# The second layer of a four-layer network: border zeros written earlier, two sampled units interleaved on VectorE, and x read back in four pieces

## The reference, cut to what matters

```python
d = layernorm_over_pixels(conv1x1(depthwise3x3(x[:, :256])))
off = conv3x3(d)                       # 18 channels: y and x shift of 9 taps
samples = bilinear(d, pixel + tap + off)   # four corners, zero outside the image
dc = einsum('bckhw,ock->bohw', samples, dc_w) + dc_b
dc = layernorm_over_channels(dc) * ln_g + ln_b
out = x * (d * sigmoid(dc)) + x * g    # g: a gate per channel from x[:, 256:]
```

## Time and profile before

| | us |
|---|---|
| median of 3 runs | 4316.83 (4311.97 to 4317.98) |
| profiled execution | 4315.14 |
| its span | 4313.3 |
| layer 1, first to last DVE output | 2752.0 to 3467.3 |
| of this the fetches and corner sums | 2900.7 to 3447.4 |

### The profile page before, as it was taken

How to read it: one execution, slowest core, us unless ns; L and a number is a source line. 1 busy time by engine, 2 the same in 40 slices (tenths; PEclk the granted TensorE clock), 3 DMA queues, 4 the chain that set the end, 5 groups by cost and what they waited for, 6 DMA issues and landing times. The chain is left out here.

```text
span 4313.3 us, 67226 instructions
## 1 busy us (share of the span) xinstructions
PE 3912.8 (91%) x18504; PEld 2390.0 (55%) x18504; DVE 2958.2 (69%) x4476; ACT 2583.8 (60%) x4599; POOL 2081.0 (48%) x1857
## 2 busy tenths in 40 slices
PE   5999999999999999999998999788779377969999
PEld 3555555555555555555557777447667242435553
DVE  7888888888888888888875333538888833235562
ACT  5899999999999999999984333222112420113331
POOL 0555555555555555555542555316676500026663
PEclk8999999999999999999999999899899677989999
DMA  1200000000000000000001000229999812453312
GB/s 48 101 10 10 9 9 12 10 9 9 12 10 9 9 12 10 9 9 12 9 24 64 0 0 0 76 82 378 369 370 392 301 46 66 142 133 69 69 40 78
DMA packets 146902, 326.60 MB, mean 76 GB/s; under 512 B 45736, under 2 KB 46760, under 8 KB 145788
## 3 DMA queue, kind: packets, MB, share of 16 engines
q1 hardware_dynamic: 105340, 174.46, 13.0%
q0 software_dynamic: 41472, 151.01, 9.0%
HBM read 246.14 MB, written 79.04 MB: 75 GB/s over the span
## 5 line engine op out<-in xcount | busy, mean ns | idle before, releaser
L559 POOL TENSOR_TENSOR cpb_sum<-cpb_tab 128x512 f32<-128x512 f32 x1028 | 1045.8, 1048 | 964.8 <-DVE cpb_r L689 964.5
L670 ACT ACTIVATE cpb_h<-cpb_z,net_vec 128x512 f32<-128x512 f32 x1536 | 1006.0, 697 | 50.2 <-PE cpb_z L610 37.5
L607 PE MATMUL cpb_z<-cpb_r,cpb_w2a 128*128 128x512 f32 x2048 | 858.2, 419 | 23.4 <-DVE cpb_h L730 23.4
L689 DVE SCALAR_TENSOR_TENSOR cpb_r<-cpb_sum,cpb_r 128x512 fp32r<-128x512 f32 x1024 | 696.2, 710 | 187.4 <-ACT cpb_r L664 187.4
L608 PE MATMUL cpb_z<-cpb_r,cpb_w2b 128*128 128x512 f32 x2048 | 801.3, 391 | 0.0
L610 PE MATMUL cpb_z<-cpb_r,cpb_w2a 128*128 128x512 f32 x2048 | 799.4, 390 | 0.0
L689 DVE SCALAR_TENSOR_TENSOR cpb_r<-cpb_z,cpb_r 128x512 fp32r<-128x512 f32 x1028 | 662.0, 686 | 160.0 <-ACT cpb_r L664 154.3
L664 ACT ACTIVATE cpb_r<-cpb_z 128x512 fp32r<-128x512 f32 x1028 | 560.4, 604 | 127.7 <-PE cpb_z L594 127.7
L664 ACT ACTIVATE cpb_r<-cpb_sum 128x512 fp32r<-128x512 f32 x1024 | 598.4, 648 | 2.0 <-POOL cpb_sum L559 2.0
L607 PEld LDWEIGHTS cpb_z<-cpb_r,cpb_w2a 128*128 128x128 f32 x2048 | 383.7, 187 | 365.9 <-issue 300.9
L1537 DVE SCALAR_TENSOR_TENSOR dc_acc<-dc_g,dc_wt,dc_acc 128x512 f32<-128x512 f32 x560 | 444.9, 800 | 57.5 <-DMA dc_g<-conv_out,dc_idx 37.0
(11 more groups left out here) (345 smaller groups left out, 5206.0 us busy)
## 6 DMA issues: line engine op xcount, KB each, us to landing
conv_out<-dc_ys SPq DMA_DIRECT2D x576, 64.0 KB
cpb_log<-log_dram SPq DMA_DIRECT2D x66, 256.0 KB, 3.1
qk_parts<-gn_r SPq DMA_DIRECT2D x64, 256.0 KB, 2.0
dc_wr<-in_dc_wT SPq DMA_DIRECT2D x9, 1024.0 KB
bias_dram<-cpb_bst SPq DMA_DIRECT2D x520, 8.0 KB
net_x<-in_x SPq DMA_DIRECT2D x8, 1024.0 KB, 9.9
sa_qa<-qk_parts SPq DMA_DIRECT2D x16, 512.0 KB
sa_ka<-qk_parts SPq DMA_DIRECT2D x16, 512.0 KB
```

The lines of the kernel that those rows point to most:

```text
L559: pool.tensor_tensor(SUM[:, r, :].rearrange("p (y x) -> p y x", x=W), TAB[:, slot, r, 0, :].unsqueeze(1).broadcast_to([P, NF // W, W]), TA ...
L607: pe.matmul(z2[:, bank, :], W2A[:], R1[:, k, :], start=True, stop=False)
L670: act.activation(H2[:, t % 8, :], z2[:, t % 3, :], ACT.Relu, bias=V("cpb_b2")).then_inc(h2a, 1)
L689: v.scalar_tensor_tensor(R2[:, t % RING, :], first_layer(t), 0.0, R1[:, t % RING, :].bitcast(F32), ALU.max, ALU.subtract).then_inc(r2_read ...
```

## The change

- The 18 border DMAs leave layer 1. SP issues them in `layer0_mlp`, from a tile of zeros of half the width there (each row is written as two halves), after a memset by POOL, and waits for them at the end of that stage. POOL's wait for the borders before the first fetch goes, and so does the memset of layer 1's ZERO.
- In layer 1 POOL zeroes only the one-pixel ring of DP that the offset convolution reads, in two memsets, instead of all of DP. PE, not ACT, waits for it.
- The four corner steps of a unit (k = 0..3) are issued skewed: in round u DVE issues step 0 of unit u, step 2 of unit u-1, step 1 of unit u, step 3 of unit u-1. Steps 0 to 2 of the first 120 units write their running sum to PSUM (`pn`, four banks), and only step 3 writes ACC. For the last 24 units the sums stay in ACC.
- x comes back in four DMAs of 1 MB: the first when PE is done, the others when 129, 136 and 140 units are sampled.

The core of the diff ("..." marks lines left out):

```diff
@@ layer0_mlp
+        ZERO = s.sb("zero", [P, C // 2])
...
+        @block.sync
+        def _(sp):
+            sp.wait_ge(blank, 1)
+            HP = H + 4
+            edge, gaps = 2 * HP + 2, H - 1
+            for rows in itertools.chain(*g["conv_out"]):
+                for r0 in (0, HP * HP - edge):
+                    sp.dma_start(rows[r0:r0 + edge, :].rearrange("r (k c) -> r k c", k=2),
+                                 ZERO[0:edge, :].unsqueeze(1).broadcast_to([edge, 2, C // 2])).then_inc(borders, 16)
+                middle = rows[edge + W:edge + W + gaps * HP, :].rearrange("(y x) c -> y x c", x=HP)[:, 0:4, :]
+                sp.dma_start(middle.rearrange("y x (k c) -> y (x k) c", k=2),
+                             ZERO[0:gaps, :].unsqueeze(1).broadcast_to([gaps, 8, C // 2])).then_inc(borders, 16)
+            sp.wait_ge(borders, 16 * 18)
...
+            pool.memset(ZERO[:], 0.0).then_inc(blank, 1)
@@ layer1
-            for u in range(SLOTS):
-                for b in range(B):
-                    rows = table[u][b]
-                    sp.dma_start(rows[0:edge, :], ZERO[0:edge, :]).then_inc(borders, 16)
...
             sp.wait_ge(y_mm, TILES)
-            sp.dma_start(X[:].rearrange("p t n -> p (t n)"), x_spill).then_inc(x_back, 16)
-            sp.wait_ge(borders, 16 * 3 * SLOTS * B)
+            for n, units in enumerate((0, LAST[1] + 1, LAST[2] - 4, LAST[3] - 4)):
+                cols = slice(n * NF, (n + 1) * NF)
+                if units:
+                    sp.wait_ge(sampled, units)
+                sp.dma_start(X[:, :, cols], x_spill.rearrange("p (t n) -> p t n", t=CT)[:, :, cols]).then_inc(x_back[n], 16)
...
-            pool.memset(DP[:], 0.0).then_inc(zeroed, 1)
+            images = DP[:].rearrange("p m b h w -> p (m b) h w")
+            pool.memset(images[:, :, 1:H + 3:H + 1, 1:W + 3], 0.0).then_inc(zeroed, 1)
+            pool.memset(images[:, :, 2:H + 2, 1:W + 3:W + 1], 0.0).then_inc(zeroed, 1)
             pool.memset(OFW[:], 0.0).then_inc(zeroed, 1)
-            pool.memset(ZERO[:], 0.0).then_inc(zeroed, 1)
...
             pool.wait_ge(idx_ready, 1)
             pool.wait_ge(gate_mm, 1)
-            pool.wait_ge(borders, 16 * 3 * SLOTS * B)
...
+            def step(w, k):
...
+                held = pn[:, w % 4, :] if w < HELD else o
+                so_far = held if k else DCB[:] if tap == 0 else o
+                if k == 0:
+                    v.wait_ge(gathered[w % GR], 32 * (w // GR + 1))
+                elif k == 3:
+                    v.wait_ge(part[2], w + 1)
+                else:
+                    v.wait_ge(part[k - 1], w + 1)
+                v.scalar_tensor_tensor(o if k == 3 else held, G[:, w % GR, k // 2, (k % 2) * C:(k % 2 + 1) * C],
+                                       WT[:, k, col:col + 1], so_far, ALU.mult, ALU.add
+                                       ).then_inc(part[k] if k < 3 else sampled, 1)
...
+            for u in range(TILES + 1):
+                if u < TILES:
+                    step(u, 0)
+                if u:
+                    step(u - 1, 2)
+                if u < TILES:
+                    step(u, 1)
+                if u:
+                    step(u - 1, 3)
```

More of the change, by code:

```diff
@@ L1 @@
 from contextlib import ExitStack
+import itertools
 import math
@@ L885, in layer0_mlp @@
         FULL = s.sb("full", [P, 2, NF])
+        ZERO = s.sb("zero", [P, C // 2])
+        blank, borders = s.sem("blank"), s.sem("borders")
         py = s.ps("py", [P, CT, NF])
@@ L1103, in layer1 @@
         GA = s.sb("ga", [P, CT, B, 2])
-        ZERO, DCB = s.sb("zero", [P, C]), s.sb("dcb", [P, C])
+        DCB = s.sb("dcb", [P, C])
         LM, LR, LN = (s.sb("lm", [P, NT, 4, 2]), s.sb("lr", [P, NT, 4]), s.sb("ln", [P, NT, 4]))
@@ L1110, in layer1 @@
         x_spill = nc.dram_tensor("x_spill", (P, CT * TOK), F32).ap()
-        table = [[nc.dram_tensor(f"conv_out{u}{b}", (HP * HP, C), F32).ap() for b in range(B)] for u in range(SLOTS)]
+        table = g["conv_out"]
         ORDER = [(tap, b) for tap in range(TAPS - 2) for b in range(B)] + [(tap, b) for b in range(B)
@@ L1130, in layer1 @@
                                                               s.sem("gate"))
-        borders, idx_ready = s.sem("borders"), s.sem("idx_ready")
+        idx_ready = s.sem("idx_ready")
         wh_ready, wl_ready = s.sem("wh_ready"), s.sem("wl_ready")
@@ L1135, in layer1 @@
         gathered = [s.sem(f"gathered{r}") for r in range(GR)]
-        part, sampled = s.sem("part"), s.sem("sampled")
+        part, sampled = [s.sem(f"part{k}") for k in range(3)], s.sem("sampled")
         l_mean, l_var, l_std, l_rstd, l_shift, normed = (s.sem("l_mean"), s.sem("l_var"), s.sem("l_std"), s.sem("l_rstd"),
@@ L1139, in layer1 @@
         n_mm, sig, d_whole, gated, x_back, x_ready = (s.sem("n_mm"), s.sem("sig"), s.sem("d_whole"), s.sem("gated"),
-                                                      s.sem("x_back"), s.sem("x_ready"))
+                                                      [s.sem(f"x_back{n}") for n in range(NT)], s.sem("x_ready"))
         block = s.block()
@@ L1145, in layer1 @@
         LAST = [(PLACE[TAPS - 1, n // 2]) * CHUNKS + (n % 2) * 4 + 4 for n in range(NT)]
+        HELD = LAST[0] - 4
         def tap_tiles(tap):
@@ L1168, in _ @@
                 sp.dma_start(OFW[:, k, :, 0:18], d["off_wT"].rearrange("t (k p) o -> k p t o", p=P)[k]).then_inc(w_in, 16)
-            edge = 2 * HP + 2
-            gaps = H - 1
-            for u in range(SLOTS):
-                for b in range(B):
-                    rows = table[u][b]
-                    sp.dma_start(rows[0:edge, :], ZERO[0:edge, :]).then_inc(borders, 16)
-                    sp.dma_start(rows[HP * HP - edge:, :], ZERO[0:edge, :]).then_inc(borders, 16)
-                    middle = rows[edge + W:edge + W + gaps * HP, :].rearrange("(y x) c -> y x c", x=HP)[:, 0:4, :]
-                    sp.dma_start(middle, ZERO[0:gaps, :].unsqueeze(1).broadcast_to([gaps, 4, C])).then_inc(borders, 16)
             weights(1)
@@ L1191, in _ @@
             sp.wait_ge(y_mm, TILES)
-            sp.dma_start(X[:].rearrange("p t n -> p (t n)"), x_spill).then_inc(x_back, 16)
-            sp.wait_ge(borders, 16 * 3 * SLOTS * B)
+            for n, units in enumerate((0, LAST[1] + 1, LAST[2] - 4, LAST[3] - 4)):
[3 more added lines that the diff above has]
+                sp.dma_start(X[:, :, cols], x_spill.rearrange("p (t n) -> p t n", t=CT)[:, :, cols]).then_inc(x_back[n], 16)
             sp.wait_ge(wr_in, 16 * TAPS)
-            sp.wait_ge(x_back, 16)
+            for n in range(NT):
+                sp.wait_ge(x_back[n], 16)
         @block.gpsimd
@@ L1259, in _ @@
             pe.wait_ge(w_in, 16 * CT)
+            pe.wait_ge(zeroed, 3)
             pe.wait_ge(d_ready, CT * B)
@@ L1334, in _ @@
                                ).then_inc(dw_ready, 1)
-            act.wait_ge(zeroed, 1)
             def weights_high(tap):
@@ L1526, in _ @@
             v.wait_ge(dcb_in, 16)
-            def sample(u, tap, b, c):
+            UNITS = [(tap, b, c) for tap, b in ORDER for c in range(CHUNKS)]
+            def step(w, k):
+                tap, b, c = UNITS[w]
                 n, q = b * 2 + c // 4, c % 4
@@ L1556, in output @@
                 cols = slice(n * NF, (n + 1) * NF)
-                if n == 0 and m == 0:
-                    v.wait_ge(x_back, 16)
+                if m == 0:
+                    v.wait_ge(x_back[n], 16)
                     v.wait_ge(gate, 1)
@@ L1562, in output @@
                                        ALU.add, ALU.mult).then_inc(x_ready, 1)
[L1564 to L1580, removed]
+            for u in range(TILES + 1):
[7 more added lines that the diff above has]
+                    step(u - 1, 3)
+                i, c = divmod(u, CHUNKS)
+                if (i, c) == (len(ORDER) - 3, 7):
+                    shifts(0)
+                elif (i, c) == (len(ORDER) - 2, 3):
+                    shifts(1)
+                elif (i, c) == (len(ORDER) - 1, 6):
+                    shifts(2)
+                if i == len(ORDER) - 2:
+                    (gated_part if c % 2 == 0 else output)(0, c // 2)
+                elif i == len(ORDER) - 1:
+                    if c < CT:
+                        gated_part(1, c)
+                    if 0 < c <= CT:
+                        output(1, c - 1)
             for m in range(CT):
@@ L2446, in build @@
             g["prefetch"], g["prefetch_done"] = prefetch, lambda sp: sp.wait_ge(pre, 16 * (CT + 2))
+            g["conv_out"] = [[nc.dram_tensor(f"conv_out{u}{b}", ((H + 4) * (H + 4), C), F32).ap() for b in range(B)]
+                             for u in range(3)]
             layer0_bias(nc, d, g)
```

## The result

The change makes the kernel slower: median 4334.32 us (4333.29 to 4342.79) against 4315.58 (4311.97 to 4317.98) for the kernel before beside it, six runs each, ratio 1.0047 [1.0034, 1.006]. The forecast was 4285, with a range of 4260 to 4303. The loss is small (0.5%) but clear of the noise, and it is a loss where a gain of 31 us was forecast. The profiled execution took 4334.47 us, its span 4332.7 against 4313.3, so the trace shows +19.4 us to account for.

A forecast was written before the change was run, and what follows sets the result against it. Bounds: POOL's memset and SP's border DMAs in front, DMA cap and DVE's pace in the loop, DVE then ACT at the end. Terms -8.2 - 15.4 + 0 - 4 - 4 = -31.6 gave 4285 us, range 4260 to 4303.

The forecast's parts named there:

- the skew in the main loop: Layer 1's loop: cheaper DVE steps offset by four buffers working like three; 0, between -20 and +20 us.
- The 4.54 us of L1210 stay: Loop, POOL's subtraction: DVE's step 0 still stops and no fetch is issued meanwhile, so no change.
- R = 3.1 us: Fetch-only phase: time per unit set by the three-deep ring, with latency L of 3.7 us from issue to data.
- In the store burst the cap sets R: Store burst: the DMAs' 413 GB/s keeps 3.49 us a unit, as long as fetch latency stays under 4.9 us.
- Rival 2: Store burst: the ring costs a little, L = 5.5, R = 3.7 us; +9 over eight taps, 4294; chance 0.16.
- Rival 3: Store burst: latency stays 7.33, R = 4.3 us, tap 64.7 against 59.0; +46, 4331, slower than before; chance 0.08.
- Memsets, -8.2: Front of layer 1: shorter POOL memsets free DVE's first operation earlier, and all 8.2 us arrive.
- Borders, -15.4: Front of layer 1: without SP's 18 DMAs weights come sooner; first fetch 23.6 us earlier, memsets included.
- x in pieces, -4: Read of x near the end: first wait 2.4 instead of 9.40 us, other three pieces 1 us each; bounds -7 and 0.
- Moved border DMAs in layer 0: Layer 0: the border DMAs are hidden by PE and cost 0; POOL's memset there 0 to +0.5 us.
- DVE's steps: Loop: skewed steps start 0.66 us apart instead of 0.78, giving 2.65 us a unit instead of 3.06 to 3.12.
- End, -4: End of layer 1: 63.8 us instead of 70.5, less 2 to 3 for the chain over ACT; bounds -7 and 0.

The follow-up runs named there:

- e1_chain: The kernel after with the four steps of a unit in a row (no skew), four G buffers; 4286.69 us, ratio 0.9931.
- e7_chain_five: The kernel after with the four steps of a unit in a row and five G buffers instead of four; 4264.23 us, ratio 0.9881.
- e2_five: The kernel after, skew kept, with five G buffers instead of four; 4276.0 us, ratio 0.9908.
- e3_before3: The kernel before with three of its four G buffers in use, memory unchanged; 4382.27 us, ratio 1.0152.
- f2_memset: The kernel before with only the short ring memsets of DP, borders written where they were; 4316.06 us, ratio 1.0001.
- f1_front: The kernel before with the front's change alone: borders written in layer 0's stage and short memsets; 4296.78 us, ratio 0.9954.
- e6_one_x: The kernel after with the four steps in a row and x read back in one DMA; 4294.34 us, ratio 0.9953.

## Why the prediction was wrong

The forecast ended on the wrong side through one term, the skew in the main loop, given as 0 between -20 and +20. It is +49.0 us from the first fetch to the end of layer 1 (609.8 against 560.8 in e1_chain). The mechanism, a ring that is one fetch shorter, was named in the prediction; what failed is what it costs behind POOL's subtraction, which was put at nothing, and in the fetch-only phase, where the latency was taken too short.

**What the skew did, piece by piece.** From the starts of step 0 on DVE's timelines a tap splits in three: the two units that begin with the one held by POOL's subtraction, the nine behind them (stores beside the fetches), and the last five (almost fetches alone). Means over the four taps from units 22, 38, 54 and 70 (21, 37, 53, 69 in e1_chain; 20, 36, 52, 68 in e7_chain_five), us:

| | two at the subtraction | nine | five | tap |
|---|---|---|---|---|
| after (skewed, four) | 12.9 | 33.7 | 17.9 | 64.5 |
| e1_chain (chained, four) | 10.4 | 32.8 | 15.7 | 58.9 |
| e7_chain_five (chained, five) | 10.5 | 29.3 | 16.1 | 55.9 |

Against e1_chain the skew adds 2.5, 0.9 and 2.1 us: 5.5 a tap in these four. Over all seven taps with a subtraction it is 43.5 us (the first and the last lose more); the rest of the 49.0 lies in the start and the end. Against my steps:

- "The 4.54 us of L1210 stay": failed, +2.5 a tap. They stay, but a wait comes on top. With one fetch fewer in the ring only one unit lies ready behind the held one, not two, and DVE is through with it before the late fetch lands. That fetch took 7.24 us, and I had not asked how many units lie ready at that moment.
- "R = 3.1 us" for fetches alone: failed in its size. The ring of three was right, but I took L = 3.7 from the very last fetch, alone in its queue. In this phase L is 4.2 to 5.1 us (a fetch whose issue ends at 3155.75 has its unit start at 3160.26), and R came to 17.9/5 = 3.6. e1_chain stays near DVE's pace, 3.1.
- "In the store burst the cap sets R", R = 3.49: held for the kernel before, and nearly for the skew. With four and with five buffers the chained order runs at 3.47 us a unit and 412 to 413 GB/s (windows under e7_chain_five), and e2_five, skewed with five, at 3.49. So it is the DMAs' pace, and the 0.37 us before every unit is its sign. That 4 R = 3.11 + 0.75 + 2.7 + 7.33 = 13.9 also gives 3.49 says nothing of a short ring, because L is mostly time in the queue: with the fifth buffer it grew from 7.6 to 11.1 us and the pace stayed. With less in flight it is otherwise. In e3_before3 the same phase moves 354 GB/s, and the skew with four 402:

```profile
3158.00:3190.00 32.00, 32.00 (x139) 25.80 (x138) 24.25 (x33) 8.30 (x13) 18.79 (x18) 1.00 0.98 354
```

```profile
3120.49:3146.64 26.15, 26.15 (x110) 20.98 (x109) 19.09 (x29) 7.82 (x12) 13.50 (x14) 0.96 1.03 402
```

That step wanted L under 4.9 us. L did sink with the shorter queue, to 5.1 to 5.9 in the last seven units of that burst, not to 3.8, and the nine units behind the subtraction average 3.7 us (3.6 in e1_chain).

Two rivals come near. Rival 2 (chance 0.16) has this burst as it came out, L = 5.5 and R = 3.7, but kept 3.1 for fetches alone and no wait behind the subtraction, and so ended at 4294. Rival 3 (chance 0.08) has the tap (64.7) and the time (4331), but by luck. It put the loss into the burst, by L at 7.33 and R at 4.3. There the skew adds 0.9 us a tap; the other 4.6 lie where rival 3 had no loss.

**The steps that held.** Front: forecast 23.6 us earlier, measured first fetch within 0.3 us of it; but the split into "Memsets, -8.2" and "Borders, -15.4" is no sum of two gains, since f2_memset gives 0 for the first, and only 18.4 us of it reach the end (f1_front). "x in pieces, -4" was -7.1 to -8.4, beyond its bound of -7, since in e1_chain the longest wait at the read is 0.97 us (against 9.33 in e6_one_x), and the three other pieces cost nothing that can be seen, where I charged 1 us each. Moved border DMAs in layer 0: layer 1 starts at 2751.18, 0.8 us earlier, and between 2751.4 and 2754.5 in the other runs that have them there (2752.0 to 2754.0 in those that have not), so no loss can be seen. DVE's steps: 0.66 us apart, as forecast. Issues of POOL: 0.94 mostly, mean 1.022.

**"End, -4"** did not come. At the read of x the wait is 3.37 us, and the last rounds still wait for fetches. From there to the last sum these waits add up to 14.7 us; before there was only the one of 9.40. (The four parts that the prediction adds up for this stretch make 63.6 and not 63.8, which changes nothing.) DVE's timeline of the kernel after:

```profile
3384.16 8.04 DVE L1560 SCALAR_TENSOR_TENSOR dc_acc<-dc_g,dc_wt,dc_acc 128x512 f32<-128x512 f32 x12 [3.37 <-DMA dc_g<-conv_out,dc_idx]
...
3458.28 2.74 DVE L1560 SCALAR_TENSOR_TENSOR dc_acc<-dc_g,dc_wt,dc_acc 128x512 f32<-128x512 f32 x4 [1.86 <-DMA dc_g<-conv_out,dc_idx]
...
3463.12 4.19 DVE L1560 SCALAR_TENSOR_TENSOR dc_acc<-dc_g,dc_wt,dc_acc 128x512 f32<-128x512 f32 x6 [1.82 <-DMA dc_g<-conv_out,dc_idx]
```

**The account.** Start of the layer -0.8, front -22.5, loop behind the new front +2.6 (569.2 in f1_front and e6_one_x, 566.6 before), pieces of x -8.4, skew +49.0, layers behind -0.5: +19.4, the difference of the spans. Where the +2.6 comes from was not tried; the same number with sums in PSUM and in ACC says that it isn't these.

**What the skew is worth with its buffer paid.** e2_five, skewed with five, has four fetches in its ring like e1_chain, chained with four, and stands at 4276.0 against 4286.7. So the cheaper steps gain 10.7 us once the lost buffer is replaced, against 22.5 that the same buffer brings when the order is left alone.

## What to carry to other kernels

Before interleaving two items on an engine that runs in order, count how many buffers are released later: a wait for item u+1 placed ahead of the release of item u takes one buffer from the ring. Here that buffer was worth 58.3 us and the cheaper operations about 11, so the reordering lost 47.6. Work out the ring (buffers x R = hold + issue + latency) with the latency found in the same phase of the trace, not from a fetch alone in its queue, and for each place where the producer stops, ask how many items lie ready when the consumer comes back. A small wait before every item (0.37 us here) can be a short ring as well as a full channel; one more buffer tells them apart. Here the pace and the wait stayed and only the latency grew, by the time of one unit: a full channel. A buffer more can still pay elsewhere, as a reserve for the places where the producer stops.

## What the runs showed of the hardware

- A chain of four steps through PSUM costs DVE the same as through SBUF: 1.55 us for two chained ones in e1_chain, 1.54 before; skewed, two of them take 1.41, and starts lie 0.66 apart against 0.79.
- The 128 x 2048 subtraction takes 4.50 to 4.65 us on POOL beside DVE and 2.28 on DVE. A DVE step that reads two SBUF tiles and falls into it took 2.60 to 5.71 us instead of 0.76.
- Indirect issues of POOL took 0.99 to 1.03 us on average when three of four DVE steps had one operand in PSUM, 1.13 to 1.15 when all read two SBUF tiles. The Trainium skill ("GPSIMD Engine Reference", "Key points") has POOL and DVE share SBUF ports for such instructions; the trace agrees. Here it was worth 3 us or less.
- The mix of 4 KB-row fetches and 2 KB-row stores ran at 412 to 413 GB/s with four or five buffers chained, at 402 skewed with four, and at 354 chained with three.
- The four DMAs of the offset weights occupy SP's queue for 9.57 us in the kernel before, 16.15 in f2_memset and 17.06 in the kernel after, as they start later or earlier; they end 20.4, 20.4 and 20.6 us after the layer's start. What in the queue ahead of them (the spill of x among it) sets that end was not tried.
